# Five of a kernel's 124 whole-tile stores are made in several transfers by rows

## What is computed

```python
def _gn(v, G=32, eps=1e-5):
    g = v.reshape(B_, G, C_ // G, H_, W_)
    m = jnp.mean(g, axis=(2, 3, 4), keepdims=True)
    s = jnp.var(g, axis=(2, 3, 4), keepdims=True)
    return ((g - m) / jnp.sqrt(s + eps)).reshape(v.shape)

def _L0_conv_ref(x):            # x is _gn(input)
    x1 = x.sum(axis=1)
    m = x1 != 0                 # n: count of m per image; pad = n.max() - n
    mean = sum_c / total        # over the places in m, per channel
    var = ...                   # of the same places
    inv = 1.0 / jnp.sqrt(var + EPS)
    xn = x * inv[None, :, None, None]
    out = jnp.where(m[:, None, :, :], xn, x)
    ...
x = x + _L0_conv_ref(_gn(x))
```

## Time and profile before

| what | us |
|---|---|
| median of 3 executions | 1269.52 |
| lowest and highest | 1268.21, 1270.65 |
| the profiled execution, its own time | 1268.77 |
| its span in the trace | 1267.1 |
| PE, DVE, ACT, POOL busy | 748.0, 784.6, 680.2, 442.9 |
| DMA: moved 537.08 MB, mean | 424 GB/s |

### The profile page before, as it was taken

One profiled execution on the slowest core, in us unless ns is written; L12 is line 12 of the kernel. 1 busy time (PEld: TensorE's weight loads), 2 busy tenths in 40 slices (PEclk: granted clock), 3 DMA queues, 4 the chain that ended last, 5 costly groups with the idle time before them and its releaser, 6 DMA issues.

```text
span 1267.1 us, 10903 instructions
## 1 busy us (share of the span) xinstructions
PE 748.0 (59%) x2882; PEld 287.2 (23%) x2882; DVE 784.6 (62%) x1926; ACT 680.2 (54%) x330; POOL 442.9 (35%) x197
## 2 busy tenths in 40 slices
PE   0776755567655576545765556655567455775556
PEld 0222222222222122221222222222122121222222
DVE  6786666565665656656566555665556655566564
ACT  0666544566435664456644466444665346654465
POOL 0044333344323443234423344333443234432340
PEclk9988776788767887678877788776887678876778
DMA  9999999999999999999999999999999999999997
GB/s 397 415 430 430 430 431 430 431 431 431 432 430 430 431 430 432 430 432 431 432 430 431 431 431 430 431 429 430 429 429 417 425 418 428 424 425 429 425 415 281
DMA packets 39042, 537.08 MB, mean 424 GB/s; under 512 B 4336, under 2 KB 4336, under 8 KB 6896
## 3 DMA queue, kind: packets, MB, share of 16 engines
q1 hardware_dynamic: 21744, 285.22, 53.2%
q10 hardware_dynamic: 17280, 251.67, 46.5%
HBM read 268.44 MB, written 268.44 MB: 424 GB/s over the span
## 4 chain that ended last, share of the span: by engine, by line
issue 54%; POOL 33%; DMA 4%; PE 3%; DVE 2%; ACT 2%; POOLq 0%; DVEq 0%; ACTq 0%; SPq 0%
POOL sums L349 31%; DMA out_dram<-slots 3%; DMA slots<-in_x_dram 2%; PE flush L457 2%; DVE stats L520 2%; ACT slots L369 1%; POOL weights L331 1%; PE stay L453 0%; PE stay L454 0%; POOL minus_mean L338 0%; PE small_ps L412 0%; ACT fresh L366 0%; POOLq L348 0%; ACT sums L366 0%; PE small_ps L425 0%
## 5 line engine op out<-in xcount | busy, mean ns | idle before, releaser
L520 DVE BATCH_NORM_STATS2 stats<-slots 128x6 f32 (+1 forms) x1024 | 619.7, 679 | 331.7 <-DMA slots<-in_x_dram 318.7
L349 POOL TENSOR_TENSOR sums<-fresh,sums 128x1536 f32<-128x1536 f32 x120 | 416.7, 3472 | 401.2 <-ACT fresh L366 401.2
L369 ACT ACTIVATE slots<-slots,outs 128x4096 f32<-128x4096 f32 (+1 forms) x140 | 489.0, 3503 | 7.9 <-PE stay L454 4.5
L457 PE MATMUL flush<-slots,weights 128*64 128x512 f32 x1488 | 416.0, 701 | 44.2 <-ACT fresh L366 42.6
L366 ACT ACTIVATE fresh<-flush,norms 128x1536 f32<-128x1536 f32 x120 | 184.1, 1534 | 144.5 <-PE flush L457 144.5
L412 PE MATMUL small_ps<-stats,group_avg 128*128 128x64 f32 x64 | 21.5, 435 | 330.3 <-DVE stats L520 330.3
L457 PEld LDWEIGHTS flush<-slots,weights 128*64 128x64 f32 x1488 | 110.9, 157 | 305.5 <-issue 181.9
L381 ACT ACTIVATE by_image<-by_image,eps 128x4 f32<-128x4 f32 x32 | 9.5, 298 | 293.7 <-DVE by_image L540 293.1
L338 POOL COPY minus_mean<-norms 128x4 f32<-128x4 f32 x32 | 6.0, 188 | 388.3 <-DVE norms L553 388.3
L453 PE MATMUL stay<-slots,weights 128*64 128x512 f32 x512 | 141.3, 618 | 0.0
L454 PE MATMUL stay<-minus_mean,weights 128*64 128x512 f32 x512 | 137.9, 593 | 0.0
(11 more groups left out here) (58 smaller groups left out, 266.4 us busy)
## 6 DMA issues: line engine op xcount, KB each, us to landing
slots<-in_x_dram SPq DMA_DIRECT2D x127, 2048.0 KB, 18.4
out_dram<-slots ACTq DMA_DIRECT2D x120, 2048.0 KB, 33.2
out_dram<-slots SPq DMA_DIRECT2D x4, 2048.0 KB, 22.6
out_dram<-slots SPq DMA_DIRECT2D x16, 512.0 KB, 5.4
slots<-in_x_dram SPq DMA_DIRECT2D x4, 512.0 KB, 16.3
```

The lines of the kernel that those rows point to most:

```text
L349: pool.tensor_tensor(sums_of(t), fresh[:, :, :], sums_of(t), ALU.add).then_inc(added, 1)
L369: return nc.scalar.activation(to, tile, ACT.Identity, bias=outs[:, u, 1, t:t + 1], scale=outs[:, u, 0, t:t + 1])
L457: nc.tensor.matmul(into, weight, source, start=True, stop=True).then_inc(image_summed, 1)
L520: last = V.bn_stats(stats[:, b * BLOCK_STATS:(b + 1) * BLOCK_STATS], slots[:, bass.ds(at + k * BLK, BLK)])
```

## The change

The stores of tiles 20, 36, 52, 68 and 84 (each the first tile of its unit, in slots 0, 6, 2, 8 and 4) are made in three or four transfers each instead of one. The list `in_parts` gives the rows of each part; the rows of a tile sum to 32. The first part has 16 rows and signals on the slot's old semaphore; the others signal on a new one, `part_stored`, and the load that reuses the slot waits for both. No other instruction is changed.

```diff
+        in_parts = {20: (16, 9, 7), 36: (16, 12, 4), 52: (16, 7, 7, 2), 68: (16, 14, 2), 84: (16, 10, 6)}
...
+        part_stored = sem("part_stored")
...
+        def part_stores(j):
+            return 16 * sum(len(in_parts[i]) - 1 for i in in_parts if i <= j)
...
                 if j >= RING:
                     sp.wait_ge(stored[j % RING], 16 * (j // RING))
+                    if j - RING in in_parts:
+                        sp.wait_ge(part_stored, part_stores(j - RING))
...
-                    act.dma_start(in_dram(out_rows, j), tile_in_ring(j)).then_inc(stored[j % RING], 16)
+                    if j in in_parts:
+                        r = 0
+                        for n in in_parts[j]:
+                            part = act.dma_start(in_dram(out_rows, j)[r:r + n, :, :], tile_in_ring(j)[r * SIDE:(r + n) * SIDE, :])
+                            if r:
+                                part.then_inc(part_stored, 16)
+                            else:
+                                part.then_inc(stored[j % RING], 16)
+                            r += n
+                    else:
+                        act.dma_start(in_dram(out_rows, j), tile_in_ring(j)).then_inc(stored[j % RING], 16)
```

More of the change, by code:

```diff
@@ L143, in norm_conv_kernel @@
         mask = held[:, 0:HALF // 2].bitcast(U8).rearrange("p (a n) -> p a n", a=HALVES)
+        in_parts = {20: (16, 9, 7), 36: (16, 12, 4), 52: (16, 7, 7, 2), 68: (16, 14, 2), 84: (16, 10, 6)}
+        assert all(sum(parts) * SIDE == P for parts in in_parts.values())
         HELD = TILES - 2 * UNIT_TILES
```

## The result

The changed kernel took 1294.35 us (median of 4, 1286.19 to 1298.43); the kernel before, beside it, 1269.64 us. The ratio is 1.0187, with a 95% interval of 1.0137 to 1.0238: 24.7 us slower by the medians. The executions of the changed kernel spread over 12 us, where the one before stays within 2.5 us. The profiled one is the slowest of the four, 1298.43 us with a span of 1296.7 us, 29.6 us longer than the span of before; sizes are therefore taken from the medians and shapes from the trace.

The account below looks back on a forecast made before the run. Bound by DMA transfers, with one slow engine last. Moving rows would end the last engine 2.1 us earlier, 1268.77 to 1266.7 us profiled; plus 0.75 us for the median gives 1267.4 us, range 1259 to 1275.

Parts of the forecast that it names:

- the straggler: One DMA engine, at 26.6 GB/s against 26.96 for the others, works alone for the last 6 us before the change.
- Its place: Which engine is last: the trace doesn't say; being among the first seven was given 0.15.
- The sum: First two engines, six rows more each, end at 1263.5 us; the last engine ends 2.1 us earlier than before.
- my first case: Straggler is the eighth engine or later; the last engine is done at 1263.2 to 1263.5 us; chance 0.55.
- the slower rival: Straggler is among the first seven engines and gets more rows: 1274 to 1284 us, 1277 if fifth; chance 0.15.
- The other rule of the Trainium skill: In the split stores, a part of n rows goes to the n lowest-numbered engines, a row each.
- Contention: First engines read partitions that others read in whole stores; at half rate 26.7 us, 1294; chance 0.03.
- The nearest rows: Whole stores and loads side by side run at full rate, so small parts were taken at full rate too.
- the first two engines: With six surplus rows each they carry 33.96 MB at 26.96 GB/s and end at 1263.5 us.
- a third row: On the first engine in a changed store, lands at most 2.43 us after its second; free while that engine isn't last.
- The costs of splitting: ACT's 11 more issues at 0.55 us, taken as 0 with 6.0 us upper bound; SP's extra wait before five loads.
- The sign by which I would have known a loaded straggler: Longer stretch at 27 GB/s, and rate below 431 soon after tile 20's store, well before 850 us.

Follow-up runs that it names:

- again4: The kernel before, with rows 1 to 4 of tiles 23, 39 and 55 stored a second time into memory that nothing reads: 1268.91 us, ratio 0.9999.
- again5: The kernel before, with rows 1 to 5 of tiles 23, 39 and 55 stored a second time: 1279.38 us, ratio 1.0077.
- probe: The kernel before, with sixteen tiny transfers behind the stores of tiles 91, 99 and 107, the k-th on k engines: 1274.55 us, ratio 1.0045.
- halves: The kernel before, with the stores of tiles 20, 36, 52, 68 and 84 in two parts of 16 rows: 1280.89 us, ratio 1.0067.
- columns: The kernel before, with the same five stores in two parts by columns, all 128 partitions each: 1269.26 us, ratio 0.9994.
- eights_high: The kernel before, with the five stores in parts of 16, 8 and 8 rows, in that order: 1306.52 us, ratio 1.0237.
- eights: The kernel before, with the five stores in parts of 8, 8 and 16 rows, in that order: 1289.45 us, ratio 1.0146.
- again16: The kernel before, with rows 1 to 16 of tiles 23, 39 and 55 stored a second time: 1276.24 us, ratio 1.0055.
- halves8: The kernel before, with eight stores, tiles 20 to 104 in steps of 12, in two parts of 16 rows: 1289.83 us, ratio 1.0156.
- only52: The kernel before, with only tile 52's store split, in parts of 16, 7, 7 and 2 rows: 1275.58 us, ratio 1.0047.
- fives: The kernel before, with the stores of tiles 36 and 68 in parts of 16, 5, 5, 5 and 1 rows: 1286.79 us, ratio 1.0132.
- fours: The kernel before, with the stores of tiles 36 and 68 in parts of 16, 4, 4, 4 and 4 rows: 1284.02 us, ratio 1.0093.
- again4_near: The kernel before, with rows 5 to 8 of tiles 23, 39 and 55 stored a second time: 1268.82 us, ratio 0.9997.
- again4_far: The kernel before, with rows 21 to 24 of tiles 23, 39 and 55 stored a second time: 1268.60 us, ratio 0.9991.
- spread6: The kernel before, with rows 1 to 4 stored a second time at six tiles (23, 35, 47, 59, 71, 83): 1276.36 us, ratio 1.0051.

## Why the prediction was wrong

**The bound and the straggler were right.** One engine sets the pace before the change. Again4 adds bytes to four engines for nothing, again5 adds the same to a fifth and loses 9.5 us. The landings show the one engine falling behind up to tile 84 and the others held to it from there, as I had read it from the rate.

**Its place was the step that failed.** The sum rests on "If the straggler is not one of them", and my first case put it behind the seventh engine. It is the fifth, which I had as the slower rival at 0.15, with +7.4 us (1277) for that place. The Trainium skill ("DMA: Bandwidth & Descriptors", "Latency and other measured facts") names engines 7 and 15, counted from 0, as the usual slow ones, and I had lowered the chance of the rival by it. In these runs it is the fifth of the engines that a small transfer takes, which is engine 4 in that count if they are taken from the lowest number on. The trace has no engine numbers, and when it can't tell, 7 places in 16 is the chance to give. The other rule of the Trainium skill that I used ("Why a DMA increments its semaphore by 16 and not by 1"), k engines, the lowest-numbered, agrees with these traces: 80 completions more, and a late engine that is in every probe from k = 5 on and in none below. The numbers themselves no trace has.

**The size was off in a second term.** The fifth place gives 7.4 to 9.5 us, of 24.7. Contention, the rival that I gave 0.03 with the words "the nearest rows, whole stores and loads side by side, run at full rate", holds most of the rest: which rows an engine reads costs time with its bytes unchanged (halves 11.1 us against columns -0.5, eights_high against eights 17 us by the medians; 147 long store packets in the changed kernel, 1 before). The nearest rows were the wrong ones: no transfer by rows is among them. That rival's figure, 1294, is what was measured, but the agreement is luck: it is half rate on the first two engines in parts of few rows alone, with nothing for the fifth engine, while halves shows a cost with no surplus at all.

**What fits.** The Trainium skill ("DMA: Bandwidth & Descriptors", "The descriptor swizzle") says which partitions each engine serves in a transfer over all 128: the fifth has rows 5 and 13 here. No run here shows that. Call any other row that it gets a foreign row. If the n engines of a part take its rows in order, then in halves it reads one foreign row per tile (row 21), in again16 and again5 none, in eights one and in eights_high two (21 and 29). Take 2.46 us for each surplus row (65.5 kB at 26.6 GB/s) and 2.3 us for each foreign one, between halves (11.1 / 5 = 2.2) and halves8 (19.9 / 8 = 2.5):

| kernel | surplus rows, foreign rows | reckoned us | measured us |
|---|---|---|---|
| again16 | 3, 0 | 7.4 | 6.3 |
| again5 | 3, 0 | 7.4 | 9.5 |
| only52 | 1, 2 | 7.1 | 5.6 |
| eights | 5, 5 | 23.8 | 19.7 |
| eights_high | 5, 10 | 35.3 | 36.0 |
| fives | 4, 6 | 23.6 | 16.3 |
| the change | 3, 8 | 25.8 | 24.7 |

By this reckoning, an estimate, the change's 25 us are 7.4 for the straggler's three rows and 18.4 for eight foreign rows. Shown are the surplus (again5 against again4) and that the rows matter with equal bytes. The rest is argued: the table fits six of seven to about 4 us and is too high for fives by 7, it can't speak of fours, where the straggler is relieved and others decide, and the order of rows within a part was not measured. And it fails where it should hold for other engines: in again4_near and again4_far the first four take three foreign rows each, by these prices 3 x (2.43 + 2.3) = 14.2 us, of which they can hide 8 to 10, and yet the time is that of before and only 5 and 8 store packets are long. So a foreign row is not slow by itself. What makes it slow in the parts of 8 and 16 rows, whether that many engines work side by side on few partitions or what else runs beside them, stays open; packets carry no engine number, so it is not shown either that the long ones are the straggler's. In the changed kernel two engines are late from tile 88 on, 13 to 25 and 16 to 26 us behind the first to land, while the other fourteen are within 5 us from tile 92 on. One may be the fifth and the other one of the first two, with six surplus rows and eleven foreign ones; nothing here says which they are.

**The other terms.** For the first two engines I had "they run at 26.96 GB/s", so that 33.96 MB end at 1263.5. That was too early: spread6 gives the first four those very bytes, and it is 6.4 us slower and not even. A sum of bytes leaves out that the ring waits for landings. I had a third row land "at most 2.43 us after its second"; in again4 a row puts the landing back by about 5. The costs of splitting that I took as zero were zero (columns), although an issue of a part takes up to 1.8 us of ACT and not 0.55. The sign by which I would have known a loaded straggler, a fall of the rate soon after tile 20's store and well before 850 us, is there in the main: 426 GB/s behind tile 20, 411 behind tile 36. The longer stretch at one engine's rate, the other half of that sign, is not: two engines are late together.

## What to carry to other kernels

Where DMA share is 1 and the last microseconds run at one engine's rate, find out which engine is last before shifting any load: tiny transfers on 1, 2, 3... engines behind a large one show it in one run. The increments of a store's semaphore show how far behind it is without any new run. Five stores in halves by rows cost 8 to 11 us even though the bytes per engine come out equal, and in halves by columns nothing, so a transfer that has to be split is split by columns here. Load can only be shifted by row parts towards the first engines here, so a straggler among them can hardly be relieved.

## What the runs showed of the hardware

- One DMA engine, the fifth, was 12 to 14 us behind the others at tiles 91 to 107, at equal bytes, and the first four had 8 to 10 us of work to spare over the kernel. A row more (64 KB) put the landing of a store back by about 5 us on its engine.
- A packet of 16 KB took 611 ns in the median. Stores' packets took at most 1.2 us before, and behind stores split by rows up to 3.9 us (over 0.9 us: 147 in the changed kernel, 1 before, from 200 to 840 us); with three transfers of four rows on top (again4_near, again4_far) only 5 and 8 of the stores' packets took over 0.9 us.
- An issue of a part by ACT took 0.58 to 1.82 us (median 0.75), an issue of a whole store 0.55.
- Executions of most kernels with row parts spread widely (12 us for the change, 22 us for eights_high, 10 us for fours, but 1.5 us for fives), while columns and again4 stayed within 2.3 us.
